# The maximum across partitions on GpSimd, the scale on all partitions at once, and no transposes on TensorE for either

## What is computed

```python
def act_quant(x):
    scale = 127.0 / jnp.clip(jnp.max(jnp.abs(x), axis=-1, keepdims=True), 1e-05, None)
    return jnp.clip(jnp.round(x * scale), -128.0, 127.0) / scale
...
scale = cond @ norm_w.T + 1.0
ms = jnp.mean(x * x, axis=-1, keepdims=True)
h = x * (scale[:, None, :] * jax.lax.rsqrt(ms + EPS))
u = h @ up_w.T
val, gate = jnp.split(u, 2, axis=-1)
h = val * jax.nn.gelu(gate, approximate=False)
hq = act_quant(h)          # straight-through in the source, the value is this
wq = weight_quant(down_w)  # ternary
y = hq @ wq.T
return y + x
```

## Time and profile before

| | |
|---|---|
| median of three runs | 789.03 us (785.71 to 789.64) |
| the profiled execution | 786.19 us |
| its span, first to last instruction | 784.4 us |
| mean granted clock of PE in it | 0.987 |
| PE busy | 758.4 us (97%), 6306 matmuls |
| DVE busy | 611.4 us (78%), 852 instructions |
| ACT busy | 428.3 us (55%), 1002 instructions |
| POOL busy | 264.4 us (34%), 318 instructions |

### The profile page before, as it was taken

One profiled execution on the slowest core, in us unless ns is written; L12 is line 12 of the kernel. 1 busy time (PEld: TensorE's weight loads), 2 busy tenths in 40 slices (PEclk: granted clock), 3 DMA queues, 4 the chain that ended last, 5 costly groups with the idle time before them and its releaser, 6 DMA issues.

```text
span 784.4 us, 17750 instructions
## 1 busy us (share of the span) xinstructions
PE 758.4 (97%) x6306; PEld 623.3 (79%) x6306; DVE 611.4 (78%) x852; ACT 428.3 (55%) x1002; POOL 264.4 (34%) x318
## 2 busy tenths in 40 slices
PE   5899998999899999999999999999999999999998
PEld 3688887888688877888788877888788877888653
DVE  5989997799867985788767985788767985775667
ACT  5688777677556543654346543654346543454233
POOL 4677975546412321224112421223112421111111
PEclk9799999999899999999999999999999999999999
DMA  6476777776695668656686658655685658465332
GB/s 207 168 262 221 252 247 236 274 268 207 175 322 196 215 182 242 240 204 169 193 304 200 214 174 246 235 210 161 199 301 200 215 172 246 172 213 179 105 132 83
DMA packets 82255, 165.50 MB, mean 211 GB/s; under 512 B 47100, under 2 KB 47652, under 8 KB 82212
## 3 DMA queue, kind: packets, MB, share of 16 engines
q1 hardware_dynamic: 81668, 164.66, 64.1%
q10 hardware_dynamic: 544, 0.27, 0.1%
HBM read 131.73 MB, written 22.17 MB: 196 GB/s over the span
## 4 chain that ended last, share of the span: by engine, by line
PE 77%; DVE 3%; DMA 2%; issue 0%; ACT 0%; SPq 0%; DVEq 0%; ACTq 0%
PE A L1209 12%; PE A L1212 12%; PE A L1211 12%; PE Y L1259 11%; PE B L1212 9%; PE B L1209 9%; PE B L1211 9%; DVE h L984 1%; DMA xT<-xf 1%; DMA wslots<-w_scratch 1%; PE X L1248 1%; DVE q L998 0%; PE S L1254 0%; PE A L1259 0%; DVE q L1007 0%
## 5 line engine op out<-in xcount | busy, mean ns | idle before, releaser
L1209 PE MATMUL A<-xT,wslots 128*128 (+1 forms) x1024 | 280.5, 274 | 7.3 <-ACT snapC L692 5.6
L1211 PE MATMUL A<-xT,wslots 128*128 (+1 forms) x1024 | 280.3, 274 | 0.0
L1212 PE MATMUL A<-xT,wslots 128*128 (+1 forms) x1024 | 280.3, 274 | 0.0
L556 POOL TENSOR_TENSOR snapC<-snapC 128x256 f32<-128x256 f32 x128 | 107.7, 841 | 447.0 <-ACT snapC L692 444.4
L1209 PE MATMUL B<-xT,wslots 128*128 (+1 forms) x768 | 210.7, 274 | 0.0
L1212 PE MATMUL B<-xT,wslots 128*128 (+1 forms) x768 | 210.7, 274 | 0.0
L1211 PE MATMUL B<-xT,wslots 128*128 (+1 forms) x768 | 210.7, 274 | 0.0
L950 DVE SCALAR_TENSOR_TENSOR h<-h,c_all,g 128x512 f32<-128x512 f32 (+1 forms) x128 | 102.8, 803 | 99.6 <-ACT g L715 99.1
L1209 PEld LDWEIGHTS A<-xT,wslots 128*128 128x128 f16 x1024 | 100.5, 98 | 24.5 <-ACT snapC L692 7.6
L1211 PEld LDWEIGHTS A<-xT,wslots 128*128 128x128 f16 x1024 | 100.6, 98 | 14.4
L1212 PEld LDWEIGHTS A<-xT,wslots 128*128 128x128 f16 x1024 | 100.7, 98 | 12.1
(11 more groups left out here) (149 smaller groups left out, 907.6 us busy)
## 6 DMA issues: line engine op xcount, KB each, us to landing
wslots<-w_scratch SPq DMA_DIRECT2D x105, 896.0 KB, 4.7
w_scratch<-wslots SPq DMA_DIRECT2D x15, 896.0 KB, 4.6
wst<-in_L_cond_up_w_dram SPq DMA_DIRECT2D x16, 512.0 KB, 6.0
xin<-in_x_dram SPq DMA_DIRECT2D x8, 1024.0 KB, 7.3
dwb<-in_L_cond_down_w_dram SPq DMA_DIRECT2D x16, 512.0 KB, 4.8
wst<-in_x_dram SPq DMA_DIRECT2D x28, 256.0 KB, 5.6
out_dram<-wst SPq DMA_DIRECT2D x28, 256.0 KB, 5.2
scl_b<-scl_rows SPq DMA_DIRECT2D x6, 256.0 KB, 7.5
```

The source lines that it names most:

```text
L556: pool.tensor_tensor(snapC[:, s % 2, 0:H], snapC[:, s % 2, 0:H], snapC[:, s % 2, H:T], ALU.add)\
L1209: pe.matmul(into, high, xh, start=(start and kp == 0), stop=False, skip_group_check=not start)
L1211: pe.matmul(into, high, xl, start=False, stop=False, skip_group_check=not start)
L1212: mm = pe.matmul(into, low, xh, start=False, stop=last, skip_group_check=not start)
```

## The change

The transposes `transpose_max` and `spread_scale` leave PE. POOL takes the maximum of `m` across the partitions with one instruction (`tokens_max`, `partition_all_reduce`) that writes the result to every partition of `mpart`; it stands in step 1 behind `gate_second(b, 0)`, and in the tail behind the last one. POOL waits for the last `largest` of the batch ahead of that `gate_second`. DVE's `quant_scale`, still in step 1, now waits for POOL and works on 128x512: clamp in `mpart`, reciprocal into the bank `S`, times 127 in `S`. The factor of the output needs the token on the partition again: a new `dequant_scale` multiplies `mpart` by the identity into `X` and reduces along the columns, in step 5 (DVE) and, in the tail, after the last clip. `q_scale` waits for `qscale_ready` in place of the transposes' signal.

```diff
@@ semaphores @@
-        amaxT_psum = sem("amaxT_psum")
+        amax_spread = sem("amax_spread")
...
-        qscale_psum = sem("qscale_psum")
@@ POOL @@
+            def tokens_max(b):
+                pool.partition_all_reduce(mpart[:, :], m[:, :], P, bass.bass_isa.ReduceOp.max).then_inc(amax_spread, 1)
...
             def batch(b, first=False, final=False):
                 for s in range(FT):
+                    if s == 1:
+                        pool.wait_ge(max_ready, MAX_OPS * b)
                     gate_second(b if s else b - 1, (s - 1) % FT)
+                    if s == 1:
+                        tokens_max(b - 1)
...
             gate_second(LAST, FT - 1)
+            pool.wait_ge(max_ready, MAX_OPS * B)
+            tokens_max(LAST)
@@ DVE @@
             def quant_scale(b):
-                dve.wait_ge(amaxT_psum, b + 1)
-                dve.tensor_reduce(qscale[:, :], X[:, :].rearrange("p (t f) -> p t f", f=P), AX.X, ALU.max)\
-                   .then_inc(amax_steps, 1)
...
+                dve.wait_ge(amax_spread, b + 1)
+                dve.tensor_scalar(mpart[:, :], mpart[:, :], QEPS, None, ALU.max).then_inc(amax_steps, 1)
+                dve.wait_ge(amax_steps, 4 * b + 1)
+                dve.reciprocal(S[:, :], mpart[:, :]).then_inc(amax_steps, 1)
+                dve.wait_ge(amax_steps, 4 * b + 2)
+                dve.tensor_scalar(S[:, :], S[:, :], QMAX, None, ALU.mult).then_inc(qscale_ready, 1)
+
+            def dequant_scale(b):
+                dve.wait_ge(amax_steps, 4 * b + 1)
+                dve.tensor_tensor(X[:, :].rearrange("p (t f) -> p t f", f=P), mpart[:, :].rearrange("p (t f) -> p t f", f=P),
+                                  ident[:, :].unsqueeze(1).to_broadcast([P, TT, P]), ALU.mult).then_inc(amax_steps, 1)
+                dve.wait_ge(amax_steps, 4 * b + 3)
+                dve.tensor_reduce(amax[:, :], X[:, :].rearrange("p (t f) -> p t f", f=P), AX.X, ALU.max)                   .then_inc(amax_steps, 1)
...
+                    if s == 5:
+                        dequant_scale(b - 1)
...
+            dequant_scale(LAST)
@@ PE @@
-            def transpose_max(b):
...
-                for t in range(TT):
-                    tr = pe.transpose(X[:, t * P:(t + 1) * P], m[:, t * P:(t + 1) * P], ident[:, :])
-                tr.then_inc(amaxT_psum, 1)
-
-            def spread_scale(b):
-                pe.wait_ge(qscale_ready, b + 1)
-                for t in range(TT):
-                    tr = pe.transpose(S[:, t * P:(t + 1) * P], qscale[:, t:t + 1].to_broadcast([P, P]), ident[:, :])
-                tr.then_inc(qscale_psum, 1)
...
-                    if s == 1:
-                        if first:
-                            pe.wait_ge(dw_steps, 1)
-                        transpose_max(b - 1)
...
-                    if s == 1:
-                        spread_scale(b - 1)
```

More of the change, by code:

```diff
@@ L169, in gated_ffn_program @@
         brow = sb("brow", [B, 1], F32)
-        ss, ms, neg_half, r_pow, r_a, r_b, rstd, amax, amax_inv, qscale = [
+        ss, ms, neg_half, r_pow, r_a, r_b, rstd, amax, amax_inv = [
             sb(n, [P, TT], F32) for n in
-            "ss ms neg_half r_pow r_a r_b rstd amax amax_inv qscale".split()]
+            "ss ms neg_half r_pow r_a r_b rstd amax amax_inv".split()]
         dq = sb("dq", [P, 2 * TT], F32)
@@ L960, in largest @@
                 if j == 0:
-                    at_least(dve, amaxT_psum, b)
-                    dve.memset(mpart[:, 0:1], 0.0)
+                    at_least(dve, amax_spread, b)
+                    dve.memset(amax_inv[:, 0:1], 0.0)
                 dve.tensor_reduce(into[:, :], h_tiles(b, first, n).rearrange("p n t -> p t n"), AX.X, ALU.max,
@@ L969, in quant_scale @@
             def quant_scale(b):
-                dve.wait_ge(amaxT_psum, b + 1)
-                dve.tensor_reduce(qscale[:, :], X[:, :].rearrange("p (t f) -> p t f", f=P), AX.X, ALU.max)\
-                   .then_inc(amax_steps, 1)
[L973 to L978, removed]
+                dve.wait_ge(amax_spread, b + 1)
[10 more added lines that the diff above has]
+                dve.tensor_reduce(amax[:, :], X[:, :].rearrange("p (t f) -> p t f", f=P), AX.X, ALU.max)                   .then_inc(amax_steps, 1)
+                dve.wait_ge(amax_steps, 4 * b + 4)
                 dve.tensor_scalar(dq_of(b, 0, TT), amax[:, :], mdq[:, 0:1], None, ALU.mult).then_inc(dq_ready, 1)
@@ L982, in q_scale @@
                 pair = h_tiles(b, 2 * PAIR_ORDER[i], 2)
-                dve.wait_ge(qscale_psum, b + 1)
+                dve.wait_ge(qscale_ready, b + 1)
                 dve.tensor_tensor(pair, pair, S[:, :].unsqueeze(1).to_broadcast([P, 2, T]), ALU.mult)\
@@ L1241, in p7 @@
                 product(BA[s % 2][:, 0:H], b, s, S3, T3, False, u3_psum)
-            def transpose_max(b):
-                pe.wait_ge(max_ready, MAX_OPS * b + MAX_OPS)
-                if is_first(b):
-                    pe.wait_ge(xf_ready, 2 * KT)
-                for t in range(TT):
-                    tr = pe.transpose(X[:, t * P:(t + 1) * P], m[:, t * P:(t + 1) * P], ident[:, :])
-                tr.then_inc(amaxT_psum, 1)
-            def spread_scale(b):
-                pe.wait_ge(qscale_ready, b + 1)
-                for t in range(TT):
-                    tr = pe.transpose(S[:, t * P:(t + 1) * P], qscale[:, t:t + 1].to_broadcast([P, P]), ident[:, :])
-                tr.then_inc(qscale_psum, 1)
             def down(b, t, bank, steps, first, last):
@@ L1365, in _ @@
             down_tile(BEFORE, 1, range(0, FT // 2))
-            transpose_max(LAST)
             down_tile(BEFORE, 1, range(FT // 2, FT))
-            spread_scale(LAST)
             down_tile(BEFORE, 2)
```

## The result

The changed kernel takes 879.5 us (median of 4 runs, 876.5 to 881.4) where the kernel before takes 788.3 (median of 4, measured beside it): a ratio of 1.117, 95% interval 1.114 to 1.120. It is 91 us slower; 872 us had been forecast, between 812 and 929. The profiled execution took 880.11 us with a span of 878.3 us and a mean granted clock of 0.943, against 786.19, 784.4 and 0.987.

What follows compares the result with a forecast made beforehand. PE was taken to bound the kernel. Stalls of 58.4 us, slower clock 18.6 and tail 6.7 added 83.7 us to the profiled 786.19, giving 869.9, or 872 us on the median's scale; range 812 to 929.

Steps and rivals of the forecast that it cites:

- What bounds it: PE bounds the kernel from the second batch on, 77% of the chain; the transposes cost it 0.96 us a batch.
- R: Time GpSimd needs to change its function library, both ways around the reduction: fetch 3.7 plus restart 1.28, 5 us.
- The rival of the free reload: Changing the library is free; Path 1 decides, 2.4 us a batch, total 809, or 812 on the median's scale; chance 0.15.
- D: Time of POOL's new 128x512 reduction, taken as three one-input passes: 4.2 us, bounds 0.78 and 9.6.
- Path 1: In step 3 PE's `p5` waits for DVE's `value(b, 1)`, late by R + D - 1.84, 7.4 us.
- The rival of the long reduction: D is 9.6 us, POOL stopping ACT and PE by the same queue: 916 us; chance 0.14, of which 0.06 beyond 929.
- DVE's passes: `quant_scale` on 128x512: clamp 0.48, reciprocal 3.4, product 0.69, with gaps 4.65 us; `dequant_scale` in step 5 costed at nothing.
- path 2: POOL's late `gate_second(b, 1)` blocks ACT, so PE's `p4` in step 3 comes 2R + D - 5.7 late, 8.5 us.
- the sign given for being right: Each batch one PE gap of some 9 us in step 3, ended by `snap_u3`, then some 5 us at half clock.
- a sign of a short reload: R is wrong if POOL's next addition follows the reduction at once and PE's gap ends by `value` instead.
- The clock, 2.65 us a stall: After each PE stall some 5.3 us at half speed lose 2.65 us; seven stalls, 18.6 us.
- The tail, 6.7 us: After the last batch the first scaling starts 6.7 us later, at 766.5, and DVE leads from there to the end.

Runs made afterwards that it cites:

- the reloads alone: The kernel before, transposes kept, plus a 128x2 reduction on GpSimd in step 1 of batches 1 to 7 whose result nobody reads: 859.7 us, ratio 1.092.
- The kernel of 781.5 us: Changed kernel rearranged in batches 2 to 7: tiny early reduction, three gate additions on DVE, wide passes later; transposes kept in batch 1 and tail: 781.5 us.
- the control: The kernel of 781.5 us with PE's transposes back in every batch, without the GpSimd reduction and DVE's wide passes: 786.2 us, ratio 0.999.

## Why the prediction held, point by point

**What bounds it: right.** PE bounds, the transposes were priced at 0.96 us a batch, and most of that gain is there wherever nobody waits: 0.8 us a batch without reloads, 0.88 with hidden ones.

**The reload, R = 5 us: there both ways, size too small.** It comes in both directions and in every batch. Ahead of the reductions it takes 7.2 us on average (5.8 in the tail, 9.2 in batch 1), on the way back 6.8 to 7.5. I had built it from the quickest load and ACT's table load; the slowest load would have been nearer, though still no measurement. No run shows the term of the forecast, a fetch of 3.7 us and a restart of 1.28, nor that a library is loaded; they show idle time beside a pair of MODIFY_POOL_CONFIG, at each change and in both directions, 7.2 us on average ahead of the reductions and 7.1 on the way back. The rival of the free reload, which rested on the earlier trace rows, is out.

**The reduction, D = 4.2 us: too large.** It takes 1.80 us, close to the two-input pass of 1.375 us and far from three passes. The two errors cancel where R and D stand together: 5 + 4.2 = 9.2 us forecast, 7.4 + 1.8 = 9.2 measured in the batch shown. Path 1 therefore came out as forecast by luck: 7.4 us late against PE's old times, and so, as PE comes 0.96 us sooner, a gap of 8.3, where 7.91 was measured. The agreement is no proof of either term. The rival of the long reduction, at D = 9.6, fell by the 1.80 us alone; a time beyond 929 us would have asked for a D above some 11 us (an estimate, from 916 us at 9.6 and eight microseconds for each further one), and no row or run shows one.

**DVE's passes: right.** The reciprocal took 3.36 us (3.4 forecast from the slope between 2 and 8 columns), the clamp 0.43 (0.48), the product 0.70 (0.69). The 0.1 us for a signal stood in no row: the clamp started 0.03 us behind the end of the reduction, and the matmul of PE that waits for `value` 0.06 us behind the end of `value`. That the reciprocal would hardly count inside the batches, since path 2 ends later, is what its removal showed; it didn't count in the tail either, which the forecast had not seen. `dequant_scale` cost nothing visible inside the batches.

**Path 2, 2R + D - 5.7: right in form, its size follows R.** Here R counts twice, so the errors don't cancel: with the measured values 14.8 + 1.8 - 5.7 = 10.9 us, not 8.5. The forecast had one gap of some 9 us ended by `snap_u3`. There are two: PE first waits for `value`, 7.91 us, and then for `snap_u3`, 3.29 us. That was to be had from the forecast's own two paths: PE runs p5 ahead of p4, so a `value` 7.4 us late stops it first, and `snap_u3` adds only the difference. The sum stands, but the sign given for being right was wrong: the longer gap ends by `value`, which the forecast had named as a sign of a short reload. Over seven batches that is 72.3 us of waiting; the forecast's 58.4 with the 6 or 7 x 0.96 us it left inside the wait makes about 65.

**The clock, 2.65 us a stall: right in kind, a little small.** 22.8 us were lost, some 2.7 of them in the tail; that leaves some 20 for the seven batches, where 18.6 had been summed. The old stall that gave the price stands late in batch 1 (206.78), not at the start of batch 2, so the array had not been without a gap from the second batch on. In the batch shown, PE is at half clock from 560.6 to 570.4, through its second gap: 6.4 us of work in place of the 5.3 of the one stall in the old trace. The profile gives the clock as a share: at 0.50 the matmuls of 256 columns behind that old stall start 0.213 us apart, 1.2 columns a nanosecond, and at 1.00 from 212.2 on 0.11 us apart.

**The tail, 6.7 us: the size right, the way partly wrong.** Timelines of DVE and of PE, answering to the earlier trace rows:

```profile
843.67 0.69 DVE L975 TENSOR_TENSOR m<-m,mpart 128x512 f32<-128x512 f32 x1
...
852.26 1.22 DVE L997 TENSOR_TENSOR h<-h,S 128x1024 f32<-128x1024 f32 x1
...
872.50 1.59 DVE L1025 SCALAR_TENSOR_TENSOR wslots<-A,dq,xin 128x512 f32<-128x512 f32 x2 [1.42 <-PE A L1261]
```

```profile
858.26 1.89 PE L1261 MATMUL A<-dT,q 128*128 128x512 f16 x4 [4.95 <-DVE q L1020]
```

The first scaling came 7.9 us after the last maximum, where it was 2.96 in the earlier trace rows: 4.9 us more and not 6.7, as reload and reduction together (5.77 + 1.80) were shorter there than R + D. But the first output came 28.1 us after that maximum, where it was 21.7: 6.5 us more. The forecast had DVE lead to the end; the chain that ended last runs over PE from 858.26 on. PE starts its last down product there after 4.95 us of waiting, and from 858.2 to 863.6 its granted clock is 0.50, with 5.34 us of work. That the total agrees is in part luck.

**The sum.** On the scale of the profiled execution 869.9 us were forecast and 880.1 measured. Of the missing 10 us, waiting in the seven batches accounts for about 7, the clock there for 1 to 2 and the small waits of batches 0 and 1 for 2; the tail as a whole came out as forecast.

## What to carry over

The reduction on GpSimd cost two reloads here, 7.2 us ahead of it and 7.1 behind it on average when it took 1.80 us itself, and 7.8 and 7.6 when it took 0.37 (the reloads alone). So what decided was not how long it takes but who waits for POOL in the 17 us around it. Look in the trace for records of MODIFY_POOL_CONFIG and for idle time with "issue" as its reason around them. The kernel of 781.5 us shows a way to use such an instruction: force the reload early with a tiny one, and give the work that others need from that engine to another for as long. When two uncertain terms only ever enter as a sum, a correct total confirms neither; the path in which one of them counts twice tells them apart.

## What the runs showed of the hardware that I had not expected

The reload at the start seems to depend on how the execution before ended. It took 0.07 us in the kernel before and 0.06 in the control, which have no reduction, 0.31 or 0.32 in the changed kernel and the six others whose last reload is a way back, and 10.3 us in the one kernel whose last reload is one ahead of a reduction.

The reload is no constant. In the version of 781.5 us it took between 8.5 and 10.8 us ahead of the reduction, with PE running through it; in the changed kernel mostly around 7. Two stretches of POOL's idle time, of that version and of the changed kernel (columns as above; the last three are granted clock, DMA share, GB/s):

```profile
401.70:411.50 9.80, 9.80 (x92) 8.78 (x91) 8.30 (x13) 5.28 (x13) 0.02 (x2) 1.00 0.98 349
```

```profile
554.80:562.20 7.40, 1.46 (x6) 0.72 (x6) 7.09 (x7) 0.00 (x0) 0.00 (x0) 0.62 0.00 0
```

Several of the long ones fall where the DMA engines are busy at 0.97 and more, and ahead of the reductions of batch 7 and of the tail, at a share of 0.16 and 0.17, it took 6.07 and 5.77 us in the changed kernel. But the longest, 10.82 us, fell at a share of 0.57; 7.38 us were enough at 0.83, and on the way back it took 7.45 at 0.00. Whether the transfers lengthen the reload was not tried and stays open.

The reduction's own time differs with the columns: 1.80 us at 128x512 in the changed kernel (1.88 in the version of 781.5 us), mostly 0.37 at 128x2.
